# Value products of two turns taken together in an image/text attention stage

## The reference, cut to what matters

```python
    def _L2_xattn_ref(x, context, q_w, q_b, k_w, k_b, v_w, v_b, k_img_w, k_img_b, v_img_w, v_img_b, o_w, o_b, norm_q_w, norm_k_w, norm_k_img_w):
...
        def attention(q, k, v):
            scale = 1.0 / jnp.sqrt(jnp.asarray(HD, q.dtype))
            scores = jnp.einsum('bqhd,bkhd->bhqk', q, k) * scale
            probs = jax.nn.softmax(scores, axis=-1)
            return jnp.einsum('bhqk,bkhd->bqhd', probs, v)
...
        q = rms_norm(linear(x, q_w, q_b), norm_q_w).reshape(B, L, NH, HD)
        k = rms_norm(linear(ctx_txt, k_w, k_b), norm_k_w).reshape(B, -1, NH, HD)
        v = linear(ctx_txt, v_w, v_b).reshape(B, -1, NH, HD)
...
        img_x = attention(q, k_img, v_img)
        txt_x = attention(q, k, v)
        out = (txt_x + img_x).reshape(B, L, DIM)
        return linear(out, o_w, o_b)
```

## Time and profile before

| | before |
|---|---|
| median of 3 runs | 3516.58 us (3516.19 to 3523.0) |
| profiled execution, its own time | 3516.98 us |
| its span in the profile | 3515.3 us |
| TensorE busy | 3259.8 us, 93% |
| VectorE busy | 2414.3 us, 69% |
| ScalarE busy | 2246.8 us, 64% |

### The profile page before, as it was taken

How to read it: one execution, slowest core, us unless ns; L and a number is a source line. 1 busy time by engine, 2 the same in 40 slices (tenths; PEclk the granted TensorE clock), 3 DMA queues, 4 the chain that set the end, 5 groups by cost and what they waited for, 6 DMA issues and landing times. The chain is left out here.

```text
span 3515.3 us, 63254 instructions
## 1 busy us (share of the span) xinstructions
PE 3259.8 (93%) x22756; PEld 2799.4 (80%) x22756; DVE 2414.3 (69%) x4811; ACT 2246.8 (64%) x5204; POOL 1552.1 (44%) x1568
## 2 busy tenths in 40 slices
PE   6868968999999999998899999887999999999989
PEld 5658967889989989997666666576899999999878
DVE  7976766877777787776777777434666666666654
ACT  3426747777777777775476676514777777777743
POOL 0003126766677667672120220102555555555534
PEclk8879989999999999999899999889999999999999
DMA  5206631211120121001201010113121121120011
GB/s 194 94 3 234 218 122 67 90 62 37 43 80 31 37 85 39 31 19 50 88 1 39 1 39 1 78 39 117 63 97 49 55 74 43 43 86 31 31 40 40
DMA packets 74455, 227.78 MB, mean 65 GB/s; under 512 B 7780, under 2 KB 29472, under 8 KB 69152
## 3 DMA queue, kind: packets, MB, share of 16 engines
q1 hardware_dynamic: 67538, 184.04, 14.8%
q0 software_dynamic: 3696, 37.68, 2.9%
q10 hardware_dynamic: 2910, 2.01, 0.2%
HBM read 178.60 MB, written 45.11 MB: 64 GB/s over the span
## 5 line engine op out<-in xcount | busy, mean ns | idle before, releaser
L1208 PE MATMUL ps<-a_v_rows,a_ring 128*128 128x129 f32 (+1 forms) x7168 | 936.7, 276 | 6.2 <-DVE a_o_rows L1615 3.8
L1567 DVE SCALAR_TENSOR_TENSOR a_peak<-ps,a_k_rstd,a_peak 128x512 f32<-128x512 f32 (+1 forms) x768 | 572.4, 745 | 522.8 <-ACT a_ring L1310 515.0
L1208 PEld LDWEIGHTS ps<-a_v_rows,a_ring 128*128 128x128 f32 (+1 forms) x7168 | 878.7, 192 | 30.9 <-ACT a_ring L1323 7.5
L1310 ACT ACTIVATE a_ring<-ps,a_k_rstd 128x512 f32<-128x512 f32 (+1 forms) x896 | 615.9, 688 | 416.6 <-PE ps L1198 372.0
L1429 POOL TENSOR_TENSOR a_ring<-a_ring,a_negb 128x512 f32<-128x512 f32 (+1 forms) x506 | 640.1, 1289 | 216.7 <-ACT a_negb L1317 209.4
L1323 ACT ACTIVATE a_ring<-a_ring 128x512 f32<-128x512 f32 (+1 forms) x896 | 563.6, 632 | 57.1 <-DVE a_ring L1604 33.1
L1196 PE MATMUL ps<-a_qt,a_kt 128*128 128x512 f32 (+1 forms) x896 | 425.5, 475 | 19.9 <-DVE a_peak L1567 14.9
L1104 PEld LDWEIGHTS ps<-a_wr,a_ct 128*128 128x128 f32 (+1 forms) x2496 | 352.5, 188 | 53.6 <-issue 13.9
L1104 PE MATMUL ps<-a_wr,a_ct 128*128 128x256 f32 (+1 forms) x2496 | 371.2, 286 | 15.0 <-DMA a_ct<-ctx_lo 13.7
L1198 PE MATMUL ps<-a_qt,a_kt 128*128 128x512 f32 (+1 forms) x896 | 355.8, 397 | 0.0
L1197 PE MATMUL ps<-a_qt,a_kt 128*128 128x512 f32 (+1 forms) x896 | 355.6, 397 | 0.0
(11 more groups left out here) (469 smaller groups left out, 6095.6 us busy)
## 6 DMA issues: line engine op xcount, KB each, us to landing
a_wr<-a_w SPq DMA_DIRECT2D x96, 512.0 KB, 4.3
a_w<-a_wr SPq DMA_DIRECT2D x32, 512.0 KB, 4.0
a_wr<-a_w SPq DMA_DIRECT2D x48, 256.0 KB, 3.9
a_ct<-ctx_hi SPq DMA_DIRECT2D x8, 1090.0 KB, 5.7
a_ct<-ctx_lo SPq DMA_DIRECT2D x8, 1090.0 KB, 8.3
f_we<-in_f_experts SPq DMA_DIRECT2D x8, 1088.0 KB, 8.7
ctx_hi<-a_ct SPq DMA_DIRECT2D x4, 1602.0 KB, 5.4
ctx_lo<-a_ct SPq DMA_DIRECT2D x4, 1602.0 KB, 9.3
```

The lines of the kernel that those rows point to most:

```text
L1208: ins = pe.matmul(m.ps[:, 6 + i // 2, (i % 2) * 256:(i % 2) * 256 + VW], slot(n)[0:r, i * P:(i + 1) * P], v_rows[u // NG % 2][0:r, t, :], ...
L1310: act.activation(slot(n)[0:r, :], m.ps[0:r, SCORE_BANKS[n % 2], :], ACT.Copy, scale=k_rstd[0:r, g % 2, t:t + 1]).then_inc(kept, 1)
L1567: dve.scalar_tensor_tensor(out=peak[0:r, :], in0=m.ps[0:r, SCORE_BANKS[n % 2], :], scalar=k_rstd[0:r, u // NG % 2, t:t + 1], in1=(slot(n - ...
```

## The change

Four things change. `values` leave the even turns: in each odd turn `n` from 3 on, `values(n - 3)` and `values(n - 2)` follow `scores(n)` directly, ahead of the turn's tasks, where before `values(n - 1)` ended each turn. The last two follow the loop. The exponentials get four buffers, and `exps(n)` waits for `values(n - 4)` instead of `values(n - 3)`. Since a group's last two `values` now come in turn 1 of the next group, TS0 moves to turn 1 (for Q = 1, 2 and 3) and OX0 to turn 2 (for Q = 1). VP12 and VP0, which overwrite value rows that the group before must have used, move from turn 0 to turn 1 (Q = 0) and from turn 1 to turn 3 (Q = 3).

```diff
--- before.py
+++ after.py
@@ -2952,23 +2952,23 @@
 
 QUAD_TURNS = {
     0: (
-        "QX0 KX0 VP12 KX1 KX2 R0 R1 R2 KX3 R3", "TS0 R4 R5 KX4 R6 QS0", "R7 KX5 R8 OX0", "R9 KX6 R10 R11",
+        "QX0 KX0 KX1 KX2 R0 R1 R2 KX3 R3", "TS0 VP12 R4 R5 KX4 R6 QS0", "R7 KX5 R8 OX0", "R9 KX6 R10 R11",
         "R12 R13 OR0 OL0 KH0", "R14 R15 R16", "R17 VP13 KL0 R18", "R19 QL0", "R20 R21", "R22 R23 R24", "KH1 R25 R26",
         "R27 R28 R29", "R30 R31", "Y0 QB0 Y1 KL1",
     ),
     1: (
-        "QX0 TS0 KX0", "KX1 KX2 OX0", "R0 R1 R2 KX3 R3 QS0 NS0", "R4 R5 KX4 QL0", "R6 R7 R8 KX5 R9", "R10 R11 R12",
+        "QX0 KX0", "TS0 KX1 KX2", "R0 R1 OX0 R2 KX3 R3 QS0 NS0", "R4 R5 KX4 QL0", "R6 R7 R8 KX5 R9", "R10 R11 R12",
         "R13 KH0 R14 KX6 NZ0", "R15 R16 KL0", "R17 KH1 R18 KP0", "R19 SQ0 KP1 R20 R21 NX0 SQ1 NL0", "R22 R23 R24",
         "R25 R26 R27", "R28 KP2 R29 R30", "R31 KP3 KL1 KN0 KP4 SQ2 SQ3 QB0 KP5 SQ4",
     ),
     2: (
-        "QP0 KX0 KX1 KP6 QX0 KX2 TS0", "R0 R1 KP7 R2 KP8 SQ5 KX3 SQ6 R3 R4", "SQ7 R5 R6 SQ8 KP9 R7 R8 R9 SQ9",
+        "QP0 KX0 KX1 KP6 QX0 KX2", "TS0 R0 R1 KP7 R2 KP8 SQ5 KX3 SQ6 R3 R4", "SQ7 R5 R6 SQ8 KP9 R7 R8 R9 SQ9",
         "KX4 R10 R11", "R12 KP10 QQ0 R13 KX5", "R14 KX6 R15 KN1 SQ10", "R16 R17 OX0", "KN2 QP1 R18",
         "R19 QQ1 R20 KP11 SQ11 SQ12 KH0 KP12 R21 QN0 KP13 R22", "SQ13 R23 QS0 R24", "XB0 R25 R26",
         "KN3 QL0 R27 R28 R29", "R30 R31", "QB0 KL0 KH1 KL1",
     ),
     3: (
-        "KX0 TS0 KX1 QX0", "VP0", "R0 R1 OX0", "R2 KX2 R3", "R4 VP1 R5 KX3 R6", "R7 R8 VP2 VP3 KX4 R9 R10",
+        "KX0 KX1 QX0", "TS0", "R0 R1 OX0", "VP0 R2 KX2 R3", "R4 VP1 R5 KX3 R6", "R7 R8 VP2 VP3 KX4 R9 R10",
         "QS0 R11 R12 R13", "R14 R15", "R16 R17", "R18 R19 VP4 KX5 KX6 QL0 R20 VP5 R21 R22", "R23 R24 VP6 R25 KH0",
         "KL0 R26 KH1 R27 R28 KL1", "", "R29 R30 VP7 VP8 R31 VP9 VP10 QB0 VP11",
     ),
@@ -3077,7 +3077,7 @@
         q_st = [st.sb(f"q_st{i}", [P, QT, QH, STK], F32R) for i in range(2)]
         qt = [st.sb(f"qt{i}", [P, 2, 2 * S], F32R) for i in range(2)]
         parts = st.sb("parts", [P, QT, QH, 3])
-        probs = [st.sb(f"probs{i}", [P, 2, 2 * S]) for i in range(3)]
+        probs = [st.sb(f"probs{i}", [P, 2, 2 * S]) for i in range(4)]
         o_t = st.sb("o_t", [P, 2 * S])
         o_n = st.sb("o_n", [P, 16, HDS])
         o_rows = st.sb("o_rows", [P, QT, D])
@@ -3326,7 +3326,7 @@
                     for h in range(QH):
                         ins = pe.matmul(m.ps[32 * h:32 * h + VW2, ACC, kind * S:(kind + 1) * S],
                                         v_rows[0:r, t, g % QUADS * QH + h, :],
-                                        probs[n % 3][0:r, h // 2, h % 2 * S:(h % 2 + 1) * S],
+                                        probs[n % 4][0:r, h // 2, h % 2 * S:(h % 2 + 1) * S],
                                         start=(t == FIRST[kind]), stop=(t == LAST[kind]), skip_group_check=True)
                     ins.then_inc(pv_done, 1)
 
@@ -3362,11 +3362,13 @@
                         does[kind](to, i)
                 for n, turn in enumerate(turns):
                     scores(n)
+                    if n > 1 and n % 2:
+                        values(n - 3)
+                        values(n - 2)
                     for kind, to, i in turn:
                         if kind in does:
                             does[kind](to, i)
-                    if n:
-                        values(n - 1)
+                values(TURNS - 2)
                 values(TURNS - 1)
                 for kind, to, i in behind:
                     if kind in does:
@@ -3449,12 +3451,12 @@
 
                 def exps(n):
                     act.wait_ge(st_ready, n + 1)
-                    if n >= 3:
-                        act.wait_ge(pv_done, n - 2)
+                    if n >= 4:
+                        act.wait_ge(pv_done, n - 3)
                     elif n == 0:
                         act.wait_ge(w_lo, 4)
                     first = 4 + 2 * (n % 2)
-                    act.activation(flat2(probs[n % 3][:, :, :]), flat2(m.ps[:, first:first + 2, :]), ACT.Exp)\
+                    act.activation(flat2(probs[n % 4][:, :, :]), flat2(m.ps[:, first:first + 2, :]), ACT.Exp)\
                        .then_inc(exp_done, 1)
 
                 does = {"W": W, "NX": NX, "SQ": SQ, "QQ": QQ, "KH": KH, "KX": KX, "QS": QS, "QX": QX, "QB": QB, "OR": OR}
```

## The result

The changed kernel takes 3527.71 us (median of 9 runs, 3520.02 to 3531.11), the kernel before 3516.58 (9 runs, 3512.35 to 3523.0): a ratio of 1.0028 with the interval [1.0018, 1.0038], so 9.8 us slower by the ratio (the two medians lie 11.1 apart). The time lies in the range, but the forecast, no measurable change, was wrong. The profiled execution of the changed kernel took 3520.02 us and is the fastest of its nine.

The account below looks back on a forecast made before the run. TensorE was taken to set the pace. Drains saved against bank waits and moved tasks gave +0.8 us in four batches; with first batch -0.7, last -1.2, end -1.0: -2.1 on 3516.98, so 3515 us, range 3503 to 3529.

Parts of the forecast that it names:

- The drain: Around each `values` block on TensorE: 0.29 us beside its own products, 32 us saved over 110 merged blocks.
- the bank wait: With three task banks, the fourth and later R wait for VectorE's maxima: five R +0.15 us, six R +0.47 a pair.
- four R: Pair of turns with two R each: nobody waits, 2.97 us against 3.26 before, -0.29.
- QB0 to `scores`: At a group's start, `scores` wait for VectorE's copy: 1.41 us after QB0, against 1.74 before.
- the four with five R or their like: Four pairs a batch whose later R wait for maxima on VectorE: +0.5 us together.
- the three dense ones: Three pairs a batch full of tasks, waiting for banks: +0.44, +0.43 and +0.22 us, together +1.1.
- the moved tasks: Four pairs a batch touched by moving VP12, TS0, OX0 and VP0: +1.0 us together.
- seven pairs with up to four R: Light pairs, a batch: these seven at -0.27 us, -1.9; three with KX or OR at -0.15, -0.4; three near 0.
- the group starts (four): Pairs at the four quads' starts, where waiting for VectorE's copy eats the merge's saving: -0.1 us a batch.
- The end of the stage: Two turns of value products fall into the wait for the last exponential: -1.0 us, once.
- the bank wait decides: Rival: even turns' R wait behind odd turns' ones, 14 pairs a batch 0.3 us worse, 3532 us; chance 0.26.
- The drain decides: Rival: other tasks give VectorE time; 110 pairs gain 0.29 us each, 3485 us, or half, 3500; chances 0.13 and 0.14.

Follow-up runs that it names:

- short maxima: Maxima of R over the first half of their keys only, part of the computation left out: 3491.92 us in the changed kernel, 3512.52 in the kernel before.
- e1: The kernel before with only the four exponential buffers and the later waits of `exps`; table and value products as before: 3517.71 us, ratio 0.9994.
- e10: As e9, with VP11 also moved from turn 13 of quad 3 into turn 0 of quad 0: 3508.50 us, ratio 0.9970 to the kernel before.
- e2: The kernel before with value products merged only inside groups, at the even turn's end; old table, three buffers: 3524.62 us, ratio 1.0016.
- e9: The kernel before with only pairs that had gained merged, the last group as in the changed kernel, four buffers: 3509.75 us, ratio 0.9972.

## Why the prediction was wrong

**The drain and the bank wait were right.** Predicted and measured at the full clock: four R 2.97 and 3.04; five R 3.60 and 3.56; six R 4.13 and 4.11; with a KX as sixth 4.26 and 4.35; with a KP between 4.66 and 4.64; no task 2.29 and 2.23. QB0 to `scores` was to be 1.41, and is, with the end of VectorE's copy 0.06 ahead of `scores`:

```profile
1860.52 0.47 PE L3251 MATMUL ps<-ident_r,a_q_st 128*128 128x128 f32 x4
...
1861.18 0.69 DVE L3643 CAST a_qt<-ps 64x512 fp32r<-64x512 f32 x1
...
1861.93 0.73 PE L3311 MATMUL ps<-a_qt,a_kt 128*128 128x512 f32 x2 [0.15 <-DVE a_qt L3643]
...
1864.34 0.51 PE L3243 MATMUL ps<-ident_r,a_k_st 128*128 128x128 f32 x4 [0.71 <-ACT a_qt L3442]
```

**The terms of the sum, a batch** (the second one): the four with five R or their like +0.5, measured +0.48; the three dense ones +1.1, measured +1.16; the moved tasks +1.0, measured +0.96. One of the dense ones, quad 1 turns 9 and 10, waits for NX0's bank and not for a maximum; the prediction shows no working for it, and its number may be right by luck. Two terms failed:

- "seven pairs with up to four R at -0.27, -1.9; three with KX or OR between at -0.15, -0.4; three near 0": these 13 pairs gave -0.8, not -2.3. Only the ones with hardly anything but R between held (-0.32, -0.21, -0.23, -0.32; with a KX -0.18, -0.26, -0.15). Quad 2 turns 7 and 8 lost 0.27: VectorE works 6.26 of 6.63 us there, 0.30 more than before, and the addition that GpSimd held up takes 0.34 more. Quad 2 turns 1 and 2 lost 0.24, quad 1 turns 7 and 8 0.19, quad 3 turns 9 and 10 0.19. With short maxima the same 13 pairs give -3.2, and these four -0.20, +0.06, -0.23 and -0.23. So what the sum left out in the light pairs was the bank wait again. The prediction had costed it by the number of R and not by all that VectorE does in the pair.
- "the group starts (four) -0.1": +0.25. With this the batch comes to +2.0, where the sum had +0.2.

The end of the stage, from the last `scores` to the end of the last `values`, was to save 1.0 and took 0.3 more (2.80 us against 2.48). The whole at the full clock is +4.6 and +0.3, about 4.9, against the predicted -2.1. By itself that is still within the 7 us that the prediction called no change.

**What the prediction had no term for is the clock.** The three profiles of the changed kernel have 10.2, 17.1 and 10.2 us at half clock in the stage, which lengthened its turns by 3.5, 6.1 and 3.4 us, 4.3 on average; two profiles of before, that of e1 and that of the order of before with short maxima have none. 4.9 + 4.3 = 9.2, against 9.8 measured. That the two agree so well is in part luck: outside the stage, where nothing was changed, the three profiles of the changed kernel take 2992.8, 3007.4 and 2996.2 us and the two of before 2998.2 and 3003.4, so a single execution scatters there by more than the whole effect. The mean granted clock of all runs points the same way: 0.9579 in the 9 of the changed kernel, 0.9593, 0.9590, 0.9592 and 0.9583 in four sets of 15 to 33 runs of before, and a difference of 0.0004 to 0.0014 in 3520 us is 1 to 5 us.

Of the rivals, "the bank wait decides" named the mechanism of most of the full-clock loss, but put it in the 14 pairs with five or more R or moved tasks (the prediction's own sum has 11 of them), at 0.3 more each. Those came out as forecast, and the light ones with other work for VectorE lost instead: 7 us against the forecast and not 17. "The drain decides" falls for full maxima; with short ones 13.4 of its 32 us are saved. That the fourth buffer costs nothing held.

What stays open is why the clock falls in nearly every variant and not in the order of before. Twelve of 14 profiles with any other order or table have such stretches (e10 and e2's first have none), four of four with the old order have none, and each of the twelve has one behind its first changed instruction. But five of the 26 stretches began ahead of it, as said above, and the mean granted clock of the runs of e9 and e10 (0.9595 and 0.9589) is that of before beside them (0.9590). So the stretches go with most changed orders; that the order sets them off is not shown, and what does is open.

## What to carry to other kernels

Work that is taken together on one engine leaves the engine that empties its banks dry for longer and then crowds it: cost such a merge pair by pair, with everything that the emptying engine does in that pair, and not by the kind of task that is most frequent there. Where buffers are few, merge where the other engine has slack and leave the dense places alone: the picked merges of e9 gained 0.28%, where all of them lost 0.28%. And a change of a few microseconds can be outweighed by stretches at half clock, so compare equal pieces at the full clock and the whole time, and trust neither alone.

## What the runs showed of the hardware

All stretches at half clock that began in the stage, 26 in 12 profiles, began in turn 0 or 1 of quad 0, or of quad 2 in the last batch, whatever the order of the value products; none began anywhere else in 224 turns. They last 3.41, 6.83 or 10.24 us. Their places are the same in all these kernels, while each profile has only some of them: the changed kernel had one at the second batch in one profile of three, and at quad 0 of the last batch in all three. Five of the 26 began in turn 0 of the first group, where every kernel still does what the kernel before does.

That VectorE's addition of two tiles in SBUF can take 0.29 or 2.04 us, by 0.01 us in its start against a GpSimd multiplication, was not expected either. Two executions of one kernel, merged there, differ with it by 0.45 us in a pair of turns at the full clock.
